# Down stage with projections: later loads of the second unit's stack, the bf16 split mostly on GpSimd, layer norm rows on ScalarE, five first-pass products per group

## What is computed

```python
x = x + 0.5 * _L0_ffn_ref(_layernorm(x, axis=-1), ...)
x = x + _L0_attn_ref(_layernorm(x, axis=-1), ...)
x = x + 0.5 * _L0_ffn_ref(_layernorm(x, axis=-1), ...)

q = (qkv @ Wq + bq).reshape(B, S, H, dh).transpose(0, 2, 1, 3)
k = (qkv @ Wk + bk).reshape(B, S, KVH, dh).transpose(0, 2, 1, 3)
v = (qkv @ Wv + bv).reshape(B, S, KVH, dh).transpose(0, 2, 1, 3)
scores = jnp.einsum('bhgqd,bhkd->bhgqk', qg, k) * scale
attn = jax.nn.softmax(scores + bias[None], axis=-1)   # causal, bias = slope * (k - q)
```

## Time and profile before

| what | value |
|---|---|
| median of 3 runs | 739.87 us (738.29 to 741.99) |
| the profiled execution, its own time | 740.43 us |
| its span in the profile | 738.6 us |
| TensorE busy | 702.6 us, 95% |
| VectorE busy | 582.3 us, 79% |
| ScalarE busy | 403.3 us, 55% |
| GpSimd busy | 112.6 us, 15% |

### The profile page before, as it was taken

The page is one execution under the profiler, slowest core; times in us unless marked ns, Lnnn a source line. Parts: engine busy times, 40 slices in busy tenths (PEclk is TensorE's granted clock), DMA queues, the critical chain, the costliest instruction groups (busy, mean ns, idle before and its releaser), DMA issues.

```text
span 738.6 us, 15927 instructions
## 1 busy us (share of the span) xinstructions
PE 702.6 (95%) x5906; PEld 365.6 (50%) x5906; DVE 582.3 (79%) x1921; ACT 403.3 (55%) x579; POOL 112.6 (15%) x122
## 2 busy tenths in 40 slices
PE   8999998967999999999999999999999889999998
PEld 4554487833344444444444444444444255554598
DVE  6976468697999999999999999999999238766311
ACT  3353332132667777776777777677777743353300
POOL 3202882110000000000000000000000002103950
PEclk9999999975899999999999999999999999999999
DMA  8014533442010011001100100110010000005531
GB/s 217 1 16 77 93 64 113 144 139 85 25 38 26 27 26 40 20 21 38 33 26 20 39 20 22 39 38 20 21 39 1 2 1 0 2 1 91 107 92 58
DMA packets 47249, 34.69 MB, mean 47 GB/s; under 512 B 13106, under 2 KB 46514, under 8 KB 47172
## 3 DMA queue, kind: packets, MB, share of 16 engines
q1 hardware_dynamic: 46596, 33.60, 18.6%
q10 hardware_dynamic: 576, 0.08, 0.1%
HBM read 23.01 MB, written 10.39 MB: 45 GB/s over the span
## 4 chain that ended last, share of the span: by engine, by line
PE 52%; DVE 13%; issue 11%; ACT 2%; DVEq 0%; ACTq 0%
PE ps L1018 49%; DVE mx L903 8%; PE ps L1023 4%; DVE mx L896 1%; ACT h_all L624 1%; DVE h_all L896 1%; DVE xn L705 1%; DVE stats L693 0%; DVE wb L923 0%; DVE mm_ L920 0%; DVE sg L838 0%; ACT osb L613 0%; DVE idle L894 0%; DVEq L133 0%; DVE mv L697 0%
## 5 line engine op out<-in xcount | busy, mean ns | idle before, releaser
L624 ACT ACTIVATE h_all<-ps 128x1024 f32<-128x1024 f32 (+3 forms) x384 | 291.3, 810 | 112.4 <-PE ps L1018 109.2
L903 DVE TENSOR_REDUCE mx<-ps 128x1 f32<-128x512 f32 (+2 forms) x352 | 223.0, 681 | 9.2 <-PE ps L1018 5.8
L1018 PE MATMUL ps<-ks,xnT_all 57*128 57x512 bf16 (+3 forms) x768 | 178.9, 337 | 15.6 <-DVE mx L896 6.4
L1018 PE MATMUL ps<-h_all,vb 128*32 128x512 f32 (+3 forms) x1536 | 163.8, 500 | 0.6 <-ACT osb L613 0.6
L1018 PE MATMUL ps<-xnT_all,ks 59*128 59x512 bf16 (+3 forms) x768 | 158.6, 331 | 3.6 <-ACT h_all L624 3.4
L896 DVE CUSTOM_DVE_ANT_0 h_all<-ps,mask_w 128x384 bf16<-128x384 f32 (+1 forms) x256 | 149.3, 618 | 2.3 <-issue 0.7
L1018 PEld LDWEIGHTS ps<-ks,xnT_all 57*128 57x128 bf16 x768 | 56.5, 94 | 143.4 <-DVE mx L896 64.9
L1018 PE MATMUL ps<-cb 64*128 64x64 bf16 (+3 forms) x1216 | 113.0, 215 | 0.0
L717 DVE TENSOR_TENSOR h_all<-ps,sg 128x512 f32<-128x512 f32 x80 | 55.2, 690 | 50.5 <-PE ps L1018 48.8
L563 ACT ACTIVATE sg<-ps 128x512 f32<-128x512 f32 x80 | 47.8, 597 | 82.6 <-PE ps L1018 82.3
L1018 PEld LDWEIGHTS ps<-cb 64*128 64x128 bf16 x1216 | 80.1, 96 | 17.3 <-issue 0.7
(11 more groups left out here) (120 smaller groups left out, 553.6 us busy)
## 6 DMA issues: line engine op xcount, KB each, us to landing
xnT_all<-q_scr SPq DMA_DIRECT2D x64, 96.0 KB
attn<-sel_scr SPq DMA_DIRECT2D x12, 256.0 KB, 7.2
mask_second<-sel_scr SPq DMA_DIRECT2D x12, 256.0 KB, 8.2
q_scr<-qp SPq DMA_DIRECT2D x8, 384.0 KB
ks<-k_scr SPq DMA_DIRECT2D x64, 48.0 KB
x<-in_x SPq DMA_DIRECT2D x8, 256.0 KB, 5.7
yT<-sel_scr SPq DMA_DIRECT2D x8, 256.0 KB, 9.0
q_scr<-qp SPq DMA_DIRECT2D x8, 256.0 KB
```

The costliest lines, as they stand in the source:

```text
L624: act.activation(pr[:, (NSTEP * i + s) % PR_BUFS, p:HPG:SLOTS, lo:HALF], ps[:, b:b + 2, lo:HALF], ACT.Exp)\
L903: dve.tensor_reduce(m, src, AX.X, V.max).then_inc(a_out, 1)
L1018: return pe.matmul(o, l, r, start=start, stop=stop, skip_group_check=True)
```

## The change

Five edits, all in the down stage with projections:

1. SyncE loads the stack of unit 1 no longer behind the stores of group 1, but one half behind the stores of group 5 and one behind those of group 6.
2. For groups 1 to 7 the split runs on GpSimd (`split_rest`: five subtractions), but for the middle part of q, one subtraction on VectorE (`middle`). Group 0 is split on VectorE as before.
3. The normalised rows of all eight groups are written by ScalarE (`rows`: four activations with scale 1/sqrt and bias `shift`), for which VectorE computes -mean/sqrt (`row_shift`, one small instruction).
4. `EARLY` and `TAIL` give 25 pieces to the groups and the tail instead of 21; groups 5 to 7 have five each instead of three.
5. The last split (now only `middle`) stands before piece 28 instead of 24.

```diff
-EARLY = [(0, 0), (0, 0), (0, 0), (0, 2), (2, 1), (2, 1), (2, 1), (2, 1)]
+EARLY = [(0, 0), (0, 0), (0, 0), (0, 0), (2, 2), (2, 3), (2, 3), (2, 3)]
-TAIL = (3, 4)
+TAIL = (3, 3)
...
-            for half in range(2):
-                load_stack(1, 1, 1, half)
             for c in range(2, GROUPS - 1):
                 store_parts(c, c // 2, c % 2)
+                if c >= GROUPS - 3:
+                    load_stack(1, 1, 1, c - (GROUPS - 3))
...
+            def split_rest(c, par):
+
+                pool.wait_ge(f1.qf, c + 1)
+                pool.tensor_tensor(qres, qf[:, :], qp[:, par, 0, :], ALU.subtract)
+                pool.wait_ge(f1.kf, c + 1)
+                pool.tensor_tensor(kres, kf[:, :], kp[:, par, 0, :], ALU.subtract)
+                parts.link(pool.tensor_tensor(kp[:, par, 1, :], kf[:, :], kp[:, par, 0, :], ALU.subtract))
+                pool.tensor_tensor(kp[:, par, 2, :], kres, kp[:, par, 1, :], ALU.subtract).then_inc(f1.pk, 1)
+                pool.wait_ge(f1.qm, c)
+                pool.tensor_tensor(qp[:, par, 2, :], qres, qp[:, par, 1, :], ALU.subtract).then_inc(f1.pq, 1)
+
             for c in range(GROUPS):
                 rsqrt(c, c % 2, f1.ve2, f1.xn2, f1.rs2)
                 if AHEAD + c < GROUPS:
                     mask_hidden(f1, 0, AHEAD + c)
+                if c > 1:
+                    split_rest(c - 1, 1 - c % 2)
+            split_rest(GROUPS - 1, 1)
...
+                def rows(c, par):
+                    after(act, f.Tb, c)
+                    act.wait_ge(f.nm, c + 1)
+                    for t in range(GT):
+                        ins = act.activation(xn[:, t, :], x[:, c * GT + t, :], ACT.Identity,
+                                             bias=shift[:, par, t:t + 1], scale=rstd[:, par, t:t + 1])
+                    ins.then_inc(f.xn2, 1)
...
                     xn_T(c, par)
+                    if not last:
+                        rows(c + 1, 1 - par)
                     qk(c, par)
...
+                def middle(c, par):
+
+                    dve.wait_ge(f.qf, c + 1)
+                    dve.tensor_tensor(qp[:, par, 1, :], qf[:, :], qp[:, par, 0, :], V.subtract).then_inc(f.qm, 1)
...
+                def row_shift(c, par):
+
+                    dve.wait_ge(f.rs2, c + 1)
+                    after(dve, f.xn2, c - 1)
+                    dve.scalar_tensor_tensor(out=shift[:, par, :], in0=mv[:, par, :, 0], scalar=-1.0,
+                                             in1=rstd[:, par, :], op0=V.mult, op1=V.mult).then_inc(f.nm, 1)
...
-                        ln_apply(c, par, f.rs2, f.Tb, f.xn2)
+                        row_shift(c, par)
                         if not first:
-                            split(c - 1, 1 - par)
+                            (middle if c > 1 else split)(c - 1, 1 - par)
                             values(c - 1, (c - 1) // 2, 1 - par)
                         early_maxima(early(c, 1))
...
                 def last_split():
-                    ch.at(LINKS * GROUPS - SPLIT_LINKS)
-                    split(GROUPS - 1, 1)
+                    middle(GROUPS - 1, 1)
```

More of the change, by code:

```diff
@@ L125 @@
             "wds", "Y", "x", "ch_up", "ch_down", "ve2", "rs2", "xn2", "Tb", "xTb", "Q", "K", "V", "qf",
-            "kf", "pq", "pk", "v", "dw0", "dw1", "out")
+            "kf", "pq", "pk", "v", "dw0", "dw1", "qm", "pch", "nm", "out")
 FfnSems = namedtuple("FfnSems", FFN_SEMS)
@@ L229, in macaron @@
         rstd = sb("rstd", [P, 2, GT])
+        shift = sb("shift", [P, 2, GT])
         idle = sb("idle", [P, 4 + HPG])
@@ L500, in _ @@
                 mask_hidden(f1, 0, c)
+            parts = Chain(pool, f1.pch)
+            def split_rest(c, par):
[7 more added lines that the diff above has]
+                pool.tensor_tensor(qp[:, par, 2, :], qres, qp[:, par, 1, :], ALU.subtract).then_inc(f1.pq, 1)
             for c in range(GROUPS):
@@ L604, in body @@
                     xn_T(c, par)
+                    if not last:
+                        rows(c + 1, 1 - par)
                     qk(c, par)
                 if qkv:
+                    rows(0, 0)
                     over_groups(body)
@@ L832, in ffn_down @@
                 LN_LINKS, SPLIT_LINKS = 2, 2
-                LINKS = LN_LINKS + SPLIT_LINKS
+                def middle(c, par):
+                    dve.wait_ge(f.qf, c + 1)
+                    dve.tensor_tensor(qp[:, par, 1, :], qf[:, :], qp[:, par, 0, :], V.subtract).then_inc(f.qm, 1)
                 def split(c, par):
@@ L859, in body @@
                     if qkv:
-                        ch.at(0 if first else LINKS * c - SPLIT_LINKS)
+                        ch.at(LN_LINKS * c + (SPLIT_LINKS if c > 1 else 0))
                         dve.wait_ge(f.x, c + 1)
```

## The result

The changed kernel takes 734.11 us (median of 5 runs, 732.87 to 735.19) against 740.01 us (5 runs, 738.29 to 741.99) in the same comparison: ratio 0.9918, 95% interval 0.99 to 0.9937. That is 5.9 us, 0.8%, faster; 731.6 were forecast, in a range from 728.5 to 737.5.

The account below looks back on a forecast made before the run. VectorE was taken to bound group 6, and ScalarE's store waits group 5. Gains of 3.6 us at D(7), 0.8 more at values(7) and 3.9 after it sum to 8.3: 739.87-8.3 = 731.6 us, range 728.5 to 737.5.

Parts of the forecast that it names:

- Loads later: Groups 4 and 5: ScalarE's store waits of 7.25 and 3.10 us go, freeing 4.54 us on VectorE once.
- The new ring: Middle groups: chain from 1/sqrt through shift, rows, q and GpSimd's split back to 1/sqrt, put at 8.0 us.
- the lock: VectorE and GpSimd subtractions from SBUF exclude each other; the second waits, GpSimd 0.65 us behind `middle`.
- D(7): Start of group 7's residual addition, forecast at 155.7 us, 3.6 earlier than 159.34.
- VectorE first: When both engines wait for `qf`, `middle` on VectorE starts before GpSimd's first subtraction, which comes 0.65 us later.
- the rival: GpSimd's subtraction starts first at `qf` and `middle` waits 1.13 us: gain 4.4 us, 735.5; chance 0.25.
- the likeliest case: VectorE starts first and the first score comes 8.3 us earlier; chance 0.45.
- The clock stays up: Rival: TensorE keeps its full clock in the last projection, which takes 2.1 us less: 729.5; chance 0.10.
- values(7): Moment of group 7's values on VectorE after the last projection, forecast at 172.2 us against 176.64.
- After values(7): From there 0.2, 13 reductions and `middle` 0.65 lead to 180.9 us against 189.24, first score near 179.3.
- The second `load_maxima`: SyncE's load for the second half's scores, behind group 7's stores (landed 183.1); maxima ready at 183.5, costing nothing.
- Attention, output projection and the second block don't change: Everything after the down stage keeps its time, so the whole 8.3 us gain reaches the end.

Follow-up runs that it names:

- middle_second: The changed kernel with `middle` behind `values` on VectorE, so that GpSimd's first subtraction starts first: 737.74 us, ratio 0.9971.
- after_again: The changed kernel measured again with no edit, on another occasion: 734.59 us, ratio 0.9924.
- fill_first: The changed kernel with idle matmuls on TensorE, 8 before piece 14 and 1 behind each of pieces 14 and 15: 732.84 us, ratio 0.9905.
- fill_all: fill_gaps with one more idle matmul behind each of the 13 pieces that follow the last projection: 738.14 us, ratio 0.9963.
- old_pieces: The changed kernel with `EARLY` and `TAIL` of the kernel before: 735.05 us, ratio 0.9926.
- fill_gaps: fill_first with 14 more idle matmuls before the transposition of the maxima: 732.66 us, ratio 0.9901.
- qk_before_rows: The changed kernel with ScalarE's writes of q and k ahead of the next group's rows: 727.88 us, ratio 0.9827.
- loads_later_only: The kernel before with only unit 1's loads moved behind the stores of groups 5 and 6: 735.63 us, ratio 0.9937.
- qk_store2_fill: qk_store2 with 6 idle matmuls ahead of the transposition of group 6: 727.52 us, ratio 0.9815.
- loads_early: The changed kernel with the later loading of unit 1 undone: 736.66 us, ratio 0.9949.
- qk_store2: qk_before_rows with group 2's stores ahead of the load of unit 0's second half in SyncE's queue: 726.30 us, ratio 0.9812.

## Why the prediction was right, and which step failed

**Loads later: right.** The k-store waits of the earlier trace rows are gone. By itself this edit is most of the change's gain.

**The new ring: right, with terms off in both directions.** Rows were put at 1.15 us to the start of q; they take 1.55 (132.76 to 134.31). The 2.8 us set down for shift, rows and q is 0.25 more than its own terms (0.2, 1.15 and 1.2) add up to, which took in part of that error; from the end of 1/sqrt to GpSimd's start it takes 3.2. The bound had been the k rows' 0.38 each, and near it they lie. The Trainium skill (page "ScalarE: Activation LUTs", section What ACT_TABLE_LOAD costs) gives an activation a fixed part that grows by 93 ns for each operand that is a column vector, and these rows have two; an estimate by its figures is 1.64 us for the four, with the overlap of neighbours that it states. This case's rows, 1.65, agree. GpSimd's 128x128 subtractions take 0.42 where I put 0.37, and its 128x512 1.16; but the lock costs 0.44, not 0.65. The split with the lock takes 4.0 us where 3.5 + 0.65 were forecast. In all the ring is 8.33 us instead of 8.0, and D(7) 0.6 us late.

**VectorE first: right.** 1.59 and 0.69 in the changed kernel, against 1.16 and 1.03 in middle_second. That run is 3.6 us above the changed kernel; the rival was forecast 3.9 above the likeliest case.

**The clock stays up: it didn't.** It falls at 153, beside a wait of TensorE of 2.02 us before piece 14, as the prediction argued against this rival. In the first profile it came back within the last projection (0.98 us for the eight matmuls behind q, 1.75 in after_again). This made up for the late D(7), so that values(7) and the first score met their forecasts to within 0.3 us is in part luck; after_again has the first score at 180.00, 0.7 late.

**After values(7): right.** 6.92 us to the first score, 7.1 forecast. The second `load_maxima` left at 183.43, forecast 183.5, and no score waited for it.

**"Attention, output projection and the second block don't change": this step failed.** The instructions don't change, but the clock at which the first of them run does. The sum was made at the first score and carried unchanged to the end. In fact 8.52 us there are 6.14 at the first transposed output. In the changed kernel's second profile 7.51 us are 5.04. That the clock is the cause is shown by fill_first: same instructions in attention, same first score as that second profile, the clock back 9 us sooner, and 2.64 us less to the output. Its median is 1.3 to 1.8 us lower, though the intervals of the ratios overlap. And it is shown by all profiles together: the later the full clock comes back behind the first score, the longer the start of attention. (The clock is read in windows of 0.5 us.) The earlier trace rows had the clock at 0.50 in 172 to 176; I priced it for the last projection and as a rival that it stays up, but not for what stands behind the first score, where the kernel before got it back after 4 us.

| run | first score | full clock back from | us behind the score | start of attention | output to end |
|---|---|---|---|---|---|
| fill_all | 187.50 | 189.5 | 2.0 | 16.20 | 532.9 |
| fill_first | 179.98 | 183.0 | 3.0 | 16.62 | 534.2 |
| old_pieces | 180.83 | 184.0 | 3.2 | 16.62 | 534.2 |
| fill_gaps | 180.21 | 183.5 | 3.3 | 16.61 | 534.1 |
| before | 187.51 | 191.5 | 4.0 | 16.77 | 534.3 |
| qk_before_rows | 174.39 | 183.0 | 8.6 | 17.82 | 534.5 |
| middle_second | 183.54 | 192.5 | 9.0 | 17.85 | 535.6 |
| loads_later_only | 183.74 | 193.0 | 9.3 | 18.04 | 532.7 |
| qk_store2_fill | 172.45 | 182.0 | 9.6 | 18.25 | 532.9 |
| after | 178.99 | 190.5 | 11.5 | 19.15 | 533.0 |
| loads_early | 182.90 | 194.5 | 11.6 | 19.22 | 532.9 |
| qk_store2 | 174.13 | 186.0 | 11.9 | 19.24 | 532.9 |
| after_again | 180.00 | 192.0 | 12.0 | 19.24 | 533.0 |

From the output to the end the profiled execution regains 1.4 us. That is the clock again: in 580 to 600 the kernel before has 0.91 and the changed one 1.00, and the two last transposed outputs come 6.6 and 7.4 us earlier. It isn't shown to belong to the change. The profiles of fill_gaps, fill_first, old_pieces, middle_second and qk_before_rows, all of them the changed kernel with an edit, fall to about 0.50 once more between 570 and 602, as the kernel before does, and these six are the ones with over 534 us in the last column. In fill_first this takes back 1.2 of its 2.64 us. But for fill_all, the kernels with this second fall are those with the earliest return of the clock, so about half of what an early return gains may be lost again; one profile for each run doesn't settle it.

So the 8.3 forecast are 8.5 at the first score, 6.1 at the first output and 7.5 at the end of the span, and 5.9 in the medians, since the profiled execution of the kernel before lies 0.4 us above its median and that of the changed one 1.2 below.

**What stays open:** what decides when the clock comes back. The table shows what its return is worth, but no run tells why it comes 2 us behind the first score in one kernel and 12 in another. It doesn't follow from how early the first score is: qk_before_rows, 6 us faster, has it back after 8.6 us, and qk_store2 after 11.9.

## What to carry to other kernels

A gain at one moment holds at the end only if what follows runs at the same clock: when the stage behind it starts earlier, look at the granted clock there, and price the stretch at both levels. When work moves to another engine, write the new ring down, instruction by instruction, and ask which of its members needn't be in it; here one line's order on ScalarE was worth as much as the five edits together. And undo single edits of a change that paid: here one of five, made alone, brings 4.7 of the 5.9 us, and of another nothing can be told in the time.

## What the runs showed of the hardware

- TensorE can be busy without a gap for long and stay at 0.50: in the changed kernel it has no wait from 175.31 on, and the clock rises in 188 to 192. In the kernel before, the last wait ends at 181.54, and it rises in the same stretch.
- With idle matmuls in the wait before piece 14 (fill_first) the clock still fell at 152, but was back at 1.00 in 156 to 160, where it had been 0.50. It fell again in the next long wait, 4.30 us for the maxima. Where it falls in spite of them they stand in the way: 738.14 us for fill_all, 729.91 in its one run with a mean clock of 0.998.
- What a late return of the clock costs: 19.15 to 19.24 us for the start of attention with 11.5 to 12.0 us of it at 0.50, and 16.61 to 16.77 with 3.0 to 4.0. Eight microseconds at the lower level cost about 2.5.
- The lock between VectorE and GpSimd works on two subtractions of SBUF operands in either order. The Trainium skill ("SBUF — State Buffer", Who interferes with whom) calls the port pair that the two share an exclusive lock, and says that a VectorE instruction with two SBUF inputs contends with a GpSimd instruction that reads SBUF. The rows agree, 1.59 and 0.88 on GpSimd, 1.03 and 1.67 on VectorE, and give the price: whoever comes second is longer by the overlap less about 0.15 us (0.43 for an overlap of 0.58, 0.46 for 0.59, 0.34 for 0.48, 0.98 for 1.13). The prediction had taken the whole 0.65.
- Four activations of 128x128 from SBUF with vectors for scale and bias take 1.65 us; one subtraction on GpSimd takes 1.16 for 128x512 and 0.42 for 128x128.
